# Two counts of TensorE raised by a drain instruction in the aggregations of a two-layer graph network

## The reference, cut to what matters

```python
msgs = edge_vals[:, None] * x[edge_src]                       # layer 0
agg = jax.ops.segment_sum(msgs, edge_dst, num_segments=N)
...
norm = dinv[src] * ew * dinv[dst]                             # layer 1, two convolutions
agg = jax.ops.segment_sum(norm[:, None] * xW[src], dst, num_segments=n_nodes)
```

## Time and profile before

| | |
|---|---|
| median of 3 runs | 3846.96 us (3844.54 to 3854.53) |
| span of the profiled execution | 4334.5 us, 487.5 above the median |
| first aggregation, first gather to last | 106.3 to 1254.4 us |
| second aggregation | 1815.0 to 2944.5 us |
| third aggregation | 2976.9 to 4114.0 us |
| PE busy, share of the span | 66% |
| POOL busy, share of the span | 58% |

### The profile page before, as it was taken

One profiled execution on the slowest core, in us unless ns is written; L12 is line 12 of the kernel. 1 busy time (PEld: TensorE's weight loads), 2 busy tenths in 40 slices (PEclk: granted clock), 3 DMA queues, 4 the chain that ended last, 5 costly groups with the idle time before them and its releaser, 6 DMA issues. The chain is left out here.

```text
span 4334.5 us, 42515 instructions
## 1 busy us (share of the span) xinstructions
PE 2842.8 (66%) x12338; PEld 2151.9 (50%) x12338; DVE 1865.2 (43%) x5797; ACT 795.6 (18%) x1977; POOL 2524.5 (58%) x2689
## 2 busy tenths in 40 slices
PE   3577767777777566646656656555476767767678
PEld 2455545555544544435545545444354555555557
DVE  6343446666646823513322222222244444444443
ACT  1111101111113223301111111100022222232230
POOL 4666666666630533666666666665666666666601
PEclk9788879888888788978878778776788888888878
DMA  5333334444432466634333333332333333333305
GB/s 156 101 111 105 108 94 121 124 128 118 120 90 87 151 200 196 208 108 119 116 101 108 108 108 107 102 98 82 89 107 108 106 107 110 103 110 109 104 21 180
DMA packets 279543, 501.74 MB, mean 116 GB/s; under 512 B 59771, under 2 KB 179969, under 8 KB 279162
## 3 DMA queue, kind: packets, MB, share of 16 engines
q0 software_dynamic: 126240, 345.85, 27.7%
q1 hardware_dynamic: 135916, 139.10, 10.4%
q10 hardware_dynamic: 17136, 13.84, 1.0%
HBM read 419.12 MB, written 79.18 MB: 115 GB/s over the span
## 5 line engine op out<-in xcount | busy, mean ns | idle before, releaser
L1401 POOL DMA_INDIRECT g<-d_t,src_i x1568 | 1506.9, 961 | 806.4 <-issue 483.4
L1473 PE MATMUL bank<-g,m 128*128 128x256 f32 (+1 forms) x4704 | 1440.7, 438 | 94.3 <-issue 45.4
L1473 PEld LDWEIGHTS bank<-g,m 128*128 128x128 f32 x4704 | 943.0, 221 | 307.3 <-issue 141.2
L1401 POOL DMA_INDIRECT g<-d_xn,src_i x784 | 766.0, 977 | 389.2 <-issue 223.7
L1426 DVE TENSOR_SCALAR m<-iota,rel_f,ew_f 128x128 f32<-128x128 f32 x2352 | 702.0, 362 | 383.3 <-DMA d_xs<-zero 170.3
L1461 PE MATMUL bank<-ident,s 128*128 128x128 f32 x588 | 144.0, 334 | 438.3 <-ACT s L1407 390.2
L1437 DVE TENSOR_TENSOR accT<-bank,accT 128x256 f32 x294 | 121.9, 415 | 628.8 <-remote 269.8
L1407 ACT ACTIVATE s<-bank 128x256 f32<-128x256 f32 (+1 forms) x294 | 111.7, 380 | 1338.4 <-DMA nb<-d_deg 435.6
L1461 PEld LDWEIGHTS bank<-ident,s 128*128 128x128 f32 x588 | 86.3, 166 | 495.2 <-ACT s L1407 425.9
L1425 DVE TENSOR_SCALAR eq<-iota,rel_f 128x128 bf16<-128x128 f32 x784 | 227.5, 290 | 182.9 <-remote 140.3
L1435 DVE TENSOR_TENSOR dinv<-bank,dinv 2x128 f32 x98 | 27.1, 276 | 319.4 <-remote 310.0
(11 more groups left out here) (386 smaller groups left out, 4235.9 us busy)
## 6 DMA issues: line engine op xcount, KB each, us to landing
g<-d_t,src_i POOLq DMA_INDIRECT x1568
side_xn<-d_xn SPq DMA_DIRECT2D x96, 256.0 KB
g<-d_xn,src_i POOLq DMA_INDIRECT x784
d_swT<-wkv SPq DMA_DIRECT2D x48, 256.0 KB
swT<-d_swT SPq DMA_DIRECT2D x24, 512.0 KB, 3.7
xt<-d_xs POOLq DMA_DIRECT2D x80, 128.0 KB, 2.9
d_ys<-y ACTq DMA_DIRECT2D x80, 128.0 KB, 2.5
x<-in_x SPq DMA_DIRECT2D x24, 256.0 KB, 2.8
```

The costliest lines, as they stand in the source:

```text
L1401: pool.indirect_dma_start(g[n % RING][:, u, 0:D], None, table, bass.IndirectOffsetOnAxis(ap=k.src_i[:, t:t + 1], axis=0)).then_inc(gathere ...
L1473: ins = pe.matmul(b[:, 0:GW], m[o][:, u, :], g[r][:, u, :], start=(u == 0), stop=(u == GT - 1 and not count))
```

## The change

The count is no longer raised by the last product itself. A drain instruction of PE follows that product and raises the count. This is done for both counts and in all three aggregations; nothing else changes, no product and no wait. The list of PE has three drains more per group, 294 per aggregation and 882 in all; no other engine's list changes, and on PE nothing but these drains is put in.

```diff
@@ -1459,7 +1459,7 @@
                     pe.transpose(k.bank[7][0:2, D:D + WIN], s[n % 2][:, D:SW], k.ident[:])
                 for c in range(C):
                     ins = pe.transpose(k.bank[7][:, c * P:(c + 1) * P], s[n % 2][:, c * P:(c + 1) * P], k.ident[:])
-                ins.then_inc(window_turned, 1)
+                pe.drain().then_inc(window_turned, 1)
 
             def tile(n, u):
                 r, o, b = n % RING, n % ONEHOTS, k.bank[n % 2]
@@ -1474,7 +1474,7 @@
                 if count:
                     ins = pe.matmul(b[:, GW:SW], eq[o][:, u, :], k.ones_b[:, 0:1], start=False, stop=(u == GT - 1))
                 if u % 4 == 3:
-                    ins.then_inc(multiplied, 1)
+                    pe.drain().then_inc(multiplied, 1)
```

## The result

| | before | after |
|---|---|---|
| median of 7 runs | 3848.22 us (3844.54 to 3854.53) | 3860.46 us (3855.31 to 3864.59) |
| span of the profiled execution | 4334.5 us | 3858.6 us |

The ratio of the times is 1.0031, with a 95% interval from 1.0021 to 1.0042: a small loss, 12.2 us, just at the size that I had called the least that this kernel's measurement can tell from none. The forecast was 3848, its range 3822 to 3915. The profiled span fell by 476 us, and the median did not follow.

A forecast was written before the change was run, and what follows sets the result against it. POOL's gathers, 20.0 us per round, were taken to bound all three aggregations and hide the drains' 379 us on PE; only +1 us at the ends was added to the median, giving 3848 us, range 3822 to 3915.

The forecast's parts named there:

- first case: Whole kernel: the time stays unchanged, 3840 to 3856 us, with a chance of 0.65.
- The 478 us of stall are the profile's own: All three aggregations: late counts stalled POOL 478 us in the profiled execution; plain runs have almost none of these stalls.
- POOL's 20.0 us set the pace: All three aggregations: POOL's 16 gathers of a round, one every 1.25 us, take longer than any other engine's work.
- one sign that I had named: First aggregation, changed kernel's profile: PE's busy time per round stays and its idle time grows by some 2.6 us.
- Half the clock only behind the profile's long idle times: PE: half-clock stretches follow long idle times that plain runs lack; at full clock a first-aggregation round takes 15.6 us.
- A drain's bubble of 0.43 us (0.28 to 0.63): PE, behind each drain: one drain costs 0.43 us, six per round 2.6 us, all 882 of them 379 us.
- Hidden under POOL's pace: PE's round in the first aggregation grows from 15.6 to 18.2 us, with the dearest drain 19.4, under POOL's 20.0.
- The ends, +1: Behind each aggregation's last gather POOL covers nothing; some two drains per aggregation show, +1 us in all.
- The sum: Whole kernel: 3856 + 1 by the profiled execution's account; taken from the median, 3848 us.
- PE as the bound: Rival, first aggregation: PE cannot use all its slack; +59 us, some 3906, or 4226 if all three are bound; chance 0.22.
- Late counts real in plain runs: Rival, ends of second and third aggregations: drains bring late counts at once; 3805 to 3835 us, chance 0.13.
- A drain that does nothing: Rival, PE: the drain raises the count no sooner or later and lets next loads run ahead; 3847 us, within the forecast.

The follow-up runs named there:

- before profiled again: The kernel before, without any edit, profiled a second time; the span of the profiled execution was 3853.5 us.
- the experiment: Every second gather left out of both kernels: 2836.57 us without drains, 3165.15 with the 882 drains, 328.6 us between them.
- the four kernels of the next paragraph with drains: The changed kernel (3860.46 us); drains on multiplied only (3863.66); two drains per place (3864.68); counts on products with bare drains behind (3866.37).
- the three without: No drains at the third aggregation's half groups: before (3848.22 us); drains on window_turned only (3847.05); the change in the first two aggregations only (3850.94).

## Why the prediction was right, and what it had not seen

*The number.* 3860.46 lies outside the 3840 to 3856 of my first case, "unchanged". The range holds it only by the stretch up to 3915 that I kept for a dear drain in the first aggregation, and that is not what happened. That the range was met is in this part luck; that the drains are hidden is not.

*The 478 us of stall are the profile's own.* Right in the main: before profiled again has the span of a plain run. But the account closed within 9 us by two errors that cancel. The two spans differ by 481 us. From first gather to last, before profiled again takes 2974, so 440 of the 481 lie in the aggregations and 41 outside. My 478 counted as stall 38 us that a plain execution has too, most of them held gathers, and left the 41 outside out.

*POOL's 20.0 us set the pace.* Right. With the pace at 1.25 us the three aggregations would take 2936; they take 2977.9 in before and 2980.0 after, the rest being mostly held gathers (34 and 36 us over 0.947 each). PE still waits for gathers in the changed kernel. The source view of L1473, before profiled again and then after (idle us, times):

```profile
  DMA g<-d_t,src_i: 872.2, 498
  DMA g<-d_xn,src_i: 382.7, 186
```

```profile
  DMA g<-d_t,src_i: 651.7, 432
...
  DMA g<-d_xn,src_i: 238.7, 147
```

1254.9 us became 890.4. The 364.5 us are where the drains' time was taken from: PE waits less for gathers because it comes to them later. For this reason one sign that I had named is false. The windows view of the first aggregation with all engines, before profiled again and then after (PE's busy time stands behind the length):

```profile
107.10:1108.20 1001.10, 770.97 (x3833) 582.69 (x3834) 616.43 (x1970) 149.08 (x347) 762.40 (x784) 0.91 0.44 129
```

```profile
108.70:1104.80 996.10, 805.52 (x3839) 588.16 (x3839) 620.28 (x1970) 148.87 (x347) 757.39 (x784) 0.91 0.45 130
```

In a round, a 49th, PE's busy time did not stay but rose from 15.7 to 16.4 us, and its idle time did not grow by 2.6 but fell from 4.7 to 3.9. With POOL's pace fixed and the busy time unchanged it could not have grown.

*Half the clock only behind the profile's long idle times.* Right in part: over whole aggregations the disturbed profile was granted 0.85, 0.78 and 0.82, but the windows of before profiled again still show 0.91, 0.89 and 0.94 and not 1. It did no harm, as PE's busy 15.7, 14.2 and 14.4 us of a round there leave the slack that I had reckoned with.

*A drain's bubble of 0.43 us (0.28 to 0.63).* A little too large. Between the last tile of a half group and the turn, before profiled again and then after:

```profile
2715.69 0.81 PE L1473 MATMUL bank<-g,m 128*128 128x256 f32 x3
2716.34 0.38 PE L1461 MATMUL bank<-ident,s 128*128 128x128 f32 x2
```

```profile
2715.28 0.41 PE L1461 MATMUL bank<-ident,s 128*128 128x128 f32 x2 [0.23 <-issue]
2716.47 0.48 PE L1473 MATMUL bank<-g,m 128*128 128x256 f32 x1 [0.78 <-DMA g<-d_t,src_i]
```

The turn followed the tile without a gap; now 0.23 us of idle "issue" stand ahead of it. From start to start of the two products the median rises from 0.216 to 0.61, so 0.39 us; from a turn to the next tile, where no gather is awaited, from 0.109 to 0.353, so 0.24. Taken for all, 588 times 0.39 and 294 times 0.24 are 300 us, against my 379 (247 to 556) and the 329 of the experiment. The 0.15 from a drain's end to the next load, for which I had no row, is 0.18 us ahead of a turn and 0.05 behind one where no gather is awaited (medians). In the second row of after PE goes on to wait 0.78 us for a gather: each half group begins with such a wait, and two of the three drains of a group stand right ahead of one.

*Hidden under POOL's pace.* Right: the drains add 291 us to the aggregations when POOL has half the work, and with all of it only what they do to the gathers.

*The ends, +1.* Between and behind the aggregations, by the edges of the windows above, lie 554.3 + 20.4 + 193.8 = 768.5 us in before profiled again and 555.9 + 19.6 + 194.4 = 769.9 in after: +1.4, from one execution each. Over the four kernels of the next paragraph with drains it is 769.4 to 771.3, over the three without 761.8 to 768.5: 4.4 us apart in the mean, of which no run tells what is the last drains' and what is scatter.

*The sum.* 3848 lacked the term that came: +10.9 us in gathers of the third aggregation, as the mean of the four kernels with drains at its half groups, 761.6, less that of the three without, 750.7. The profiled spans of the same kernels differ by 16.4 us in the mean, so these 10.9 are two thirds of it; the ends' 4.4 are most of the rest. I had written that DVE and ACT get their counts later "but within the slack of 5 us", and took slack to be free. DVE's lateness by itself was free; the new places of its operations against the gathers' starts were not.

*The Trainium skill's rule* ("PSUM — Partial Sum Buffer", "Engine vs sequencer instructions") to attach the increment to the producer is one of correctness on the page, with no price, and the page names a drain as the carrier of a standalone barrier; it does not speak against the change as I had put it. The price of the 882 drains is 329 us with half the gathers, and 12 here.

*The rivals.* PE as the bound: fell with POOL's waits, which are the same in both kernels, and with the rounds of 13.6 to 15.9 us of the kernel with half the gathers. Late counts real in plain runs: fell with the second profile of before. A drain that does nothing: fell with the 0.39 us.

## What to carry to other kernels

An engine that sets the pace hides any cost on the others that fits its slack, but what is hidden still moves the others' work in time; look which of their instructions can hold the pacing engine, and where they then fall. Where DVE works beside gathers that GpSimd issues, operations with two SBUF operands are best kept short or fed from PSUM: cutting seven of them into pieces brought 14 us by the medians (a ratio of 0.9969) here, about what the change cost. And profile a kernel twice before its stalls are believed.

## What the hardware showed that I had not expected

- An indirect gather is held by a DVE operation with two SBUF operands that began at least 0.05 us before it, to the operation's end less 0.126 us. One that begins later leaves the gather at 0.95 us (L1317 above), and if it begins from 0.045 us before the gather's start to 0.02 us behind it, it is itself put off by up to 0.08 us. This fits L1317 and L1332; L635, which begins right behind another operation without a wait, held gathers that had started up to 0.03 us before it.
- Pieces of a `scalar_tensor_tensor` that follow each other at 0.20 us, each 0.27 long, can hold a gather like one operation (L638 above), and pieces of L747 at the same distance did not.
- A second drain behind the first takes 13 ns. The source view of it:

```profile
L1479 PEldq DRAIN  x588: 13/13/135, 119.5 to 3676.6; - x196
```

- With half the gathers PE kept a granted clock of 0.99 to 1.00, the 2.4 GHz level, over whole aggregations, where with all of them, and PE waiting for gathers in between, the windows above show 0.89 to 0.94.
